# The first attention layer's kept table in whole gathered rows of 266 words, one run a batch

## What is computed

```python
h = (x @ W).reshape(n, HEADS, HID)            # HEADS = 4, HID = 64
a_src = jnp.einsum('nhf,hf->nh', h, att_src)
a_dst = jnp.einsum('nhf,hf->nh', h, att_dst)
e = jax.nn.leaky_relu(a_src[src] + a_dst[dst], NEG_SLOPE)
m = jax.ops.segment_max(e, dst, num_segments=n)
ex = jnp.exp(e - m[dst])
denom = jax.ops.segment_sum(ex, dst, num_segments=n)
alpha = ex / denom[dst]
msg = h[src] * alpha[:, :, None]
agg = jax.ops.segment_sum(msg, dst, num_segments=n)
```

## Time and profile before

| what | value |
|---|---|
| time, median of 3 runs | 9093.38 us (9089.47 to 9102.39) |
| span of the profiled execution, first to last instruction | 9046.9 us |
| busy in the span | PE 63%, DVE 64%, ACT 25%, POOL 71% |
| DMA queue q1 (issued by SP) | 968942 packets, 1098.82 MB, 40.7% of 16 engines' span |
| DMA queue q0 (POOL's gathers and scatters) | 153312 packets, 296.65 MB, 17.0% |
| `source_maximum`, first to last gather | 2454 to 3597 us |
| `attend_pairs`, first to last load of rows | 3635 to 4191 us |

### The profile page before, as it was taken

The page is one execution under the profiler, slowest core; times in us unless marked ns, Lnnn a source line. Parts: engine busy times, 40 slices in busy tenths (PEclk is TensorE's granted clock), DMA queues, the critical chain, the costliest instruction groups (busy, mean ns, idle before and its releaser), DMA issues. The chain is left out here.

```text
span 9046.9 us, 131904 instructions
## 1 busy us (share of the span) xinstructions
PE 5679.9 (63%) x35786; PEld 4627.8 (51%) x35874; DVE 5810.5 (64%) x15100; ACT 2292.8 (25%) x3456; POOL 6454.7 (71%) x5675
## 2 busy tenths in 40 slices
PE   0990024444488887698344442555559898989896
PEld 0440023333333333566333332555549898989896
DVE  9660035555577666556444446555559898989898
ACT  2000000000100000343222222222226565656564
POOL 4777767777377776674677772777758787878785
PEclk6995555555655555899666666887769999999998
DMA  1780035555599999895333342444457676767674
GB/s 40 289 308 2 2 84 131 131 131 131 101 213 211 210 210 183 263 290 168 88 82 81 80 73 67 128 129 128 130 118 221 191 221 189 219 190 222 190 221 142
DMA packets 1122974, 1403.89 MB, mean 155 GB/s; under 512 B 276858, under 2 KB 948302, under 8 KB 1109198
## 3 DMA queue, kind: packets, MB, share of 16 engines
q1 hardware_dynamic: 968942, 1098.82, 40.7%
q0 software_dynamic: 153312, 296.65, 17.0%
HBM read 1010.93 MB, written 383.96 MB: 154 GB/s over the span
## 5 line engine op out<-in xcount | busy, mean ns | idle before, releaser
L2437 PE MATMUL ps<-u,wide_r 128*128 x9280 | 1140.5, 277 | 129.3 <-issue 88.6
L2268 POOL TENSOR_TENSOR msg_r<-zo_r,share_r 128x1024 f32<-128x1024 f32 x580 | 1123.1, 1936 | 101.7 <-DVE share_r L2327 46.1
L2437 PEld LDWEIGHTS ps<-u,wide_r 128*128 128x128 f32 x9280 | 1092.2, 193 | 131.3 <-issue 131.2
L2449 PE MATMUL ps<-msg_r,hots_r 128*128 128x128 f32 x9280 | 1140.7, 276 | 24.4 <-POOL msg_r L2268 23.1
L2010 POOL DMA_INDIRECT z_r<-x_tab,src_row x880 | 854.4, 971 | 417.2 <-issue 268.0
L2449 PEld LDWEIGHTS ps<-msg_r,hots_r 128*128 128x128 f32 x9280 | 1081.8, 192 | 32.9 <-POOL msg_r L2268 31.9
L297 POOL DMA_INDIRECT rec_tab<-pay,row_i x831 | 808.0, 972 | 374.9 <-issue 275.1
L575 POOL DMA_INDIRECT ring<-y_tab,y_row x880 | 838.0, 952 | 306.9 <-issue 266.0
L1172 POOL DMA_INDIRECT ring_m<-t_tab,src_row x880 | 835.3, 949 | 307.9 <-issue 280.8
L1624 POOL DMA_INDIRECT ring_e<-t_tab,src_row x880 | 832.4, 946 | 271.7 <-issue 268.0
L2276 POOL TENSOR_TENSOR prod_r<-prod_r 128x512 f32<-128x512 f32 x580 | 735.0, 1267 | 319.2 <-DVE prod_r L2299 302.9
(11 more groups left out here) (303 smaller groups left out, 10622.4 us busy)
## 6 DMA issues: line engine op xcount, KB each, us to landing
zo_r<-zo_tab SPq DMA_DIRECT2D x2320, 192.0 KB, 2.8
ring_e<-k_tab SPq DMA_DIRECT2D x464, 260.0 KB
k_tab<-ring_m SPq DMA_DIRECT2D x220, 520.0 KB, 6.3
y_tab<-wide SPq DMA_DIRECT2D x100, 1024.0 KB, 3.9
zo_tab<-z_r SPq DMA_DIRECT2D x110, 512.0 KB, 3.6
hot_bytes_e<-hb_tab SPq DMA_DIRECT2D x464, 64.0 KB, 3.3
dl_b<-dl_tab SPq DMA_DIRECT2D x220, 128.0 KB, 3.8
zo_tab<-hot_bytes SPq DMA_DIRECT2D x220, 128.0 KB
```

What stands on the lines that cost most here:

```text
L2268: nc.gpsimd.tensor_tensor(msg[:, g % WR].rearrange("p c (k d) -> p c k d", d=CD), z_of(g).rearrange("p c (k d) -> p c k d", d=CD), share[: ...
L2437: last = nc.tensor.matmul(ps[:, 2 * (g % 2) + c // 4, c % 4 * D:(c % 4 + 1) * D], wide[:, g % WR, c, :], u[:, bass.ds(tiles[g % NO % 4 * O ...
L2449: last = nc.tensor.matmul(ps[:, 4 + g % 2, c // 2 * D:(c // 2 + 1) * D], hots[:, g % WR, c, :], msg[:, g % WR, c, :], start=c % 2 == 0, st ...
```

## The change

The kept table gets rows of 266 words in place of 260. The store takes the ring's slot as it lies, split scores included, so that a partition's 4 x 260 words in pieces become one run of 1064 words in SBUF and in HBM (in the program's own listing the DMA's shape goes from 128x4x260 to 128x1064, 220 times). The ring of `attend_pairs` has rows of 266 words too, and a pair's load goes from 128x520 to 128x532 words, 464 times. Nobody reads the 6 words more in `attend_pairs`. No instruction is added, removed or moved on any engine; the line numbers behind line 1302 grow by one.

```diff
-        k1_tab = nc.dram_tensor("k1_tab", [P, NCH, HEADS * F1 + HEADS], fp32, kind="Internal").ap()
+        k1_tab = nc.dram_tensor("k1_tab", [P, NCH, HEADS * F1 + HEADS + SPLIT_W], fp32, kind="Internal").ap()
...
                             sp.dma_start(keep_tab[:, bass.ds(q * CQ, CQ), :],
-                                         ring[:, s, :, 0:W]).then_inc(s_keep[s], 16)
+                                         ring[:, s]).then_inc(s_keep[s], 16)
...
             W = hf + HEADS
+            KW = W + SPLIT_W
...
-                ring = sb(f"ring_{name}", [P, ZR, OP, 2, W], fp32, ph)
+                ring = sb(f"ring_{name}", [P, ZR, OP, 2, KW], fp32, ph)
```

## The result

The changed kernel takes 9020.88 us (median of four runs, 9015.56 to 9025.15), the kernel before 9094.90 us beside it: a ratio of 0.9917, with a 95% interval of 0.9904 to 0.9931. That is 74 us less, three times the forecast 23 and outside the range, which ended at 9050. The profiled execution of the changed kernel has a span of 9019.7 us and a time of 9021.5. So 1.8 us lie outside a span, not 46.5, and between the two traces the span fell by 27.2 us, close to the forecast.

What follows compares the result with a forecast made beforehand. POOL's gathers, held by late stores of the kept table, were taken to bound `source_maximum`. Terms -22 - 4 + 3 = -23 us on the span of 9046.9 gave 9023.9; with 46.5 added, 9070 us, range 9050 to 9101.

Steps and rivals of the forecast that it cites:

- What bounds the stage: In `source_maximum`, POOL's gathers set the pace; late stores of the kept table add waits, 39.1 us including one of 13.48.
- The store's price: Store in `source_maximum`: longer runs cut engine time from 487 to 400 us, between 302 and 503.
- The waits: POOL's waits in `source_maximum` without the long one: 22 of 25.9 us vanish.
- The drain: End of `source_maximum`, where last gathers fetch one row for slots without edges: 4 us less, between 0 and 13.2.
- The loads: Row loads of `attend_pairs`: 1.9% more bytes, mostly beside SP's issue, cost 3 us more (0 to 10).
- The signs: If right: q1 below 38%, POOL idle near 285 us, at most four gaps before 3550, last pack 20 to 30 us earlier.
- The 46.5 us: Whole kernel: the runs' median lies 46.5 us above the profiled span; added unchanged to the forecast span of 9023.9.
- No change: Rival: gathers, not stores, set the waits in `source_maximum`, so only added bytes count: 9097 us; chance 0.25.
- Turns between the queues: Slower rival: gather packets wait behind longer store packets, quads land 1.7 us later, 32 us more, 9125 us; chance 0.10.
- The long run is not cut up: Rival on the store: the long run goes out in pieces of about 1 KB, leaving only added bytes, 9097 us; chance 0.03.

Runs made afterwards that it cites:

- before_again: The kernel before, unchanged, run again for its spread: 9037.4 us, 3.1 below the kernel before in its session.
- control: The kernel before with the kept table three unused partitions' parts longer, parts still 915200 bytes apart: 9058.6 us, 3.8 below its before.
- spread_before: The kernel before with slots without edges naming 128 different rows, one a partition, in place of one row: 9028.7 us, 74.4 below its before.
- pitch_before: The kernel before, 1040-byte runs kept, with only the partitions' parts of the kept table moved to 936320 bytes apart: 9008.1 us, 35.6 below its before.
- long_915200: The changed kernel, 4256-byte runs, with parts 915200 bytes apart and only 860 of 880 chunks stored: 9016.6 us, 86.5 below its before.
- flat_915200: The kernel before with its table written as one flat row a partition, parts still 915200 bytes apart: 9100.5 us, 2.6 below its before.
- short_915264: The kernel before, 1040-byte runs, with parts 915264 bytes apart, 64 more than before: 9016.8 us, 29.3 below its before.
- spread: The changed kernel with slots without edges naming 128 different rows, one a partition, in place of one row: 8950.6 us, ratio 0.9902 to the kernel before.
- after_again: The changed kernel itself, run again in a later session: 9007.9 us, 35.8 below the kernel before.
- pieces: The changed kernel with ring rows 268 words apart, so the same words are stored in four 1064-byte runs a partition: 9012.3 us, 28.3 below its before.
- run 333: Not a follow-up run: 333 ns is SP's median time to issue a row load that is one run a partition, against 383 for two.

## Why the prediction was wrong

*What bounds the stage* was right: POOL's pace with the second layer's gathers as its floor, and waits for a late store above it. All 16 short gaps went when the store's price fell, and none came in their place. The prediction read two of the 17 gaps; in all 17 the pack was done 6.6 us or more before, and 15 lie before a quad's first gather, where POOL waits for the store. Two of the short ones (1.87 us at 2598.37, 2.04 at 3264.90) lie before a second gather, which waits for no store; what held those is not shown. The time to a store's landing bears the reading out: at the median 6.3 to 7.5 us in the traces of the old rows at 915200 bytes that show it (before, before_again, control, spread_before), 4.6 to 4.7 with the same runs at other distances.

*The store's price* had the wrong cause, and its size was too high. The prediction put the 4.20 us a MB down to short runs beside gathers and took 400 us of engine time, between 302 and 503. It came to 0.298 x 1127 = 336, and the cause is the pair of short run and distance. The change takes away both: its longer row moves the parts of the table, and it joins the runs. Either alone suffices (pitch_before, and long_915200 with the reserve made there). The prediction never looked at the distance between partitions. It also held the gathers at 0.541 x 1156 = 625 us; they fell to 0.424 x 1127 = 478, and no trace shows why. Part of it comes with the distance alone: 5.3 us a MB in flat_915200, 4.4 in short_915264.

*The waits*: forecast 22 of 25.9 us, measured 27.0 us of idle time less, 25.9 of them all of the short gaps. *The drain*: forecast 4; the gap of 13.48 came back as three of 2 to 8, together 0.5 us less, and the last pack comes 10.3 in place of 13.8 us behind the last gather's start, so 4.0 in all. spread showed that its cause, reads of one row, was right. *The loads*: forecast 3 us more, 1.7 by the two traces, which is less than this stage varies.

*The signs.* The signs named for being right came true in the changed kernel's trace: q1's share at 29.8%, 280.9 us of idle time, one gap before 3550 us, the last pack 29.5 us earlier (a store's landing does not show in that trace; in after_again, the same kernel, it takes 3.2 us at the median). None of them could tell the run's length from the distance, and the first run that could (pieces) spoke against the length. That the span fell by 27.2 us where 23 were forecast is therefore luck as to the cause.

*The 46.5 us* is the step that failed and that put the time outside the range. The prediction took the difference between the runs' median and the profiled span for time outside the span and carried it over to the changed kernel. Every run since has 1.7 to 1.9 us there. The page came from an execution with 39 us of waits, whose time, by these 1.8 us, was near 9048.7; the timed ones took 9089 to 9102. No trace of those exists, but flat_915200 at 9099.75 has the same table and 362.4 - 271.6 = 91 us of waits over the second layer's floor. So the term to be removed was, as an estimate, 39 + 46.5 - 1.8 = 84 us in the runs by which the change was measured, not 39; the changed kernel's trace still has 280.9 - 271.6 = 9 of them, and the 75 between come to the measured 74. That all of the 46.5 us were waits of this stage is not shown. Read as a warning, the 46.5 us would have said: the time varies, and something inside the span with it.

*The rivals.* No change: the time fell by 74 us. The rule of the Trainium skill ("DMA: Bandwidth & Descriptors", section "Specifications"), by which runs of 512 B and more lose nothing, would have given no change. At another distance the runs agree with it as far as time goes (9008.1 and 9007.9 us), though the 1040-byte runs still cost 3.0 us a MB against 2.8; the section does not speak of the distance. Turns between the queues: the opposite was seen, the gathers are cheaper beside the long runs (q0 at 0.401 x 1000 / 109.14 = 3.67 us a MB in after_again, 4.36 in pitch_before). The long run is not cut up: 31680 packets on q1, where before it had 114920.

## What to carry to other kernels

When a store is dearer per MB than others of the same kernel, vary the distance between the rows that are written side by side before explaining it by the length of the runs; 64 bytes of padding are a cheap experiment. Do not take the gap between a profiled span and the median of the runs for overhead: here the time outside the span was 1.8 us and the rest was time that varies, so the gain was to be had in the median, not in the page. Padding entries that all point at one row make a slow gather: spread them.

## What was not expected of the hardware

- Runs of 1040 bytes to 128 places 915200 bytes apart cost 4.15 to 4.77 us a MB on q1 (the highest in spread_before, 0.478 x 1000 / 100.12); 64 bytes more between the places give 3.01, and runs of 4256 bytes at the same distance 2.79. Gathers from another table beside them cost 5.0 to 5.3 us a MB, and 4.4 or 3.8 then.
- The same kernel's waits at that distance differ by session, 308 to 362 us of idle time at the gathers, on one chip too (333.6 in control, 362.4 in flat_915200); with them gone the times lie between 9005 and 9029 us.
- A gather of 128 equal row numbers drains at 12.5 us a MB; with 128 different rows no gap is left at the end of the stage, and the kernel with its four stages that gather is 57 us faster.
- A load in two runs a partition takes SP 383 ns to issue, one in a single run 333.
